# A four-layer graph network on one core: the second norm's squares move to ScalarE, and a score enters the first layer's gather

## The reference

```python
x = _layernorm(x + _L0_gnn_ref(x, adj, ...))   # (x Wq)(x Wk)^T times adj^T, row-normalized, times x Wv
x = _layernorm(x + _L1_gnn_ref(x, adj, ...))   # D^-1/2 adj D^-1/2 x W + b
x = _layernorm(x + _L2_gnn_ref(x, adj, ...))   # three gated steps: a = adj h; z, r sigmoids, tanh; h = (1-z) h + z hv
x = _layernorm(x + _L3_gnn_ref(x, adj, ...))   # masked attention of 8 heads, softmax, output projection
```

## Time and profile before

| what | us |
|---|---|
| median of 3 executions | 2118.96 |
| lowest and highest | 2114.54, 2122.32 |
| the profiled execution, its own time | 2114.17 |
| its span in the trace | 2112.4 |
| TensorE busy | 2027.2 |
| VectorE busy | 1570.5 |
| ScalarE busy | 1253.7 |
| GpSimd busy | 1032.5 |

### The profile page before, as it was taken

One profiled execution on the slowest core, in us unless ns is written; L12 is line 12 of the kernel. 1 busy time (PEld: TensorE's weight loads), 2 busy tenths in 40 slices (PEclk: granted clock), 3 DMA queues, 4 the chain that ended last, 5 costly groups with the idle time before them and its releaser, 6 DMA issues.

```text
span 2112.4 us, 34482 instructions
## 1 busy us (share of the span) xinstructions
PE 2027.2 (96%) x12214; PEld 1632.8 (77%) x12214; DVE 1570.5 (74%) x3442; ACT 1253.7 (59%) x2501; POOL 1032.5 (49%) x1153
## 2 busy tenths in 40 slices
PE   6889999999999999999999999999999999999986
PEld 5667787877878787787877878787787877878764
DVE  5567777777777778777777777778777777877756
ACT  3335647566575656646566575656657566565745
POOL 3123645446364554545445463554535555454546
PEclk8999999999999999999999999999999999999999
DMA  4003022120211203112120212213012120302212
GB/s 135 1 20 70 21 51 51 41 71 21 57 35 48 63 22 71 39 41 51 41 71 21 64 27 57 54 31 71 30 41 51 41 71 21 70 21 61 51 47 65
DMA packets 65631, 101.14 MB, mean 48 GB/s; under 512 B 11440, under 2 KB 31152, under 8 KB 65456
## 3 DMA queue, kind: packets, MB, share of 16 engines
q1 hardware_dynamic: 65456, 98.87, 18.4%
HBM read 23.34 MB, written 8.39 MB: 15 GB/s over the span
## 4 chain that ended last, share of the span: by engine, by line
PE 88%; DVE 4%; ACT 3%; POOL 2%; issue 2%; SPq 0%; DMA 0%; POOLq 0%; DVEq 0%; ACTq 0%
PE ps L1026 18%; PE ps L1028 17%; PE ps L1027 17%; PE ps L1048 12%; PE ps L1140 10%; PE ps L1160 6%; PE ps L1124 5%; PE ps L1451 2%; ACT fa L449 1%; POOL fa L334 1%; PE ps L1220 1%; PE ps L1253 1%; POOL rsum L328 1%; DVE ra L943 0%; DVE fa L781 0%
## 5 line engine op out<-in xcount | busy, mean ns | idle before, releaser
L328 POOL TENSOR_TENSOR rsum<-esum,mhalf 128x2 f32<-128x2 f32 x256 | 209.9, 820 | 598.6 <-ACT fa L449 598.5
L334 POOL TENSOR_SCALAR fa<-fa,rsum 128x512 f32<-128x512 f32 x512 | 442.1, 875 | 54.5 <-POOL rsum L328 54.5
L781 DVE CUSTOM_DVE_ANT_0 fa<-ps,mask 128x512 f32<-128x512 f32 x512 | 332.2, 686 | 157.3 <-PE ps L1124 152.0
L449 ACT ACTIVATE fa<-fa,nmax 128x512 f32<-128x512 f32 x512 | 367.0, 725 | 48.2 <-DVE nmax L781 48.2
L444 ACT COPY pT<-ps 128x512 f32<-128x512 f32 x480 | 276.8, 583 | 150.3 <-PE ps L1140 148.5
L1140 PE MATMUL ps<-ident,fa 128*128 128x128 f32 x1920 | 287.2, 275 | 14.6 <-POOL fa L334 10.6
L1140 PEld LDWEIGHTS ps<-ident,fa 128*128 128x128 f32 x1920 | 230.4, 141 | 88.1 <-issue 22.7
L768 DVE TENSOR_TENSOR ra<-ps,ra 128x512 fp32r<-128x512 f32 x224 | 150.9, 686 | 181.8 <-ACT ra L591 94.4
L1048 PE MATMUL ps<-adjT,ra 128*128 128x512 f32 x1024 | 261.2, 405 | 8.0 <-DVE ra L943 5.2
L1048 PEld LDWEIGHTS ps<-adjT,ra 128*128 128x128 f32 x1024 | 192.5, 192 | 63.1 <-ACT pT L444 8.3
L323 POOL TENSOR_TENSOR rstd<-veps,mhalf 128x2 f32<-128x2 f32 x128 | 98.0, 771 | 167.9 <-DVE veps L748 167.9
(11 more groups left out here) (197 smaller groups left out, 4682.8 us busy)
## 6 DMA issues: line engine op xcount, KB each, us to landing
ra<-ra SPq DMA_DIRECT2D x512, 128.0 KB, 2.4
fa<-in_x_T SPq DMA_DIRECT2D x17, 512.0 KB, 4.7
fa<-in_x SPq DMA_DIRECT2D x17, 512.0 KB, 3.9
out<-fa SPq DMA_DIRECT2D x15, 512.0 KB, 3.0
fa<-in_L_gnn_w_w SPq DMA_DIRECT2D x3, 512.0 KB, 10.7
adj_n<-in_adj SPq DMA_DIRECT2D x1, 1024.0 KB, 8.1
fa<-in_L_gnn_u_w SPq DMA_DIRECT2D x2, 256.0 KB, 10.0
out<-xn SPq DMA_DIRECT2D x2, 256.0 KB, 2.1
```

The source lines that it names most:

```text
L328: nc.gpsimd.tensor_tensor(rsum[:, 2 * k:2 * k + 2], esum[:, 2 * k:2 * k + 2], mhalf[:, 4:6], ALU.pow).then_inc(rs_r, 1)
L334: nc.gpsimd.tensor_scalar(SC[:, g], SC[:, g], rsum[:, 2 * k + u:2 * k + u + 1], 1.0, ALU.mult, ALU.mult).then_inc(nrm, 1)
L449: nc.scalar.activation(SC[:, s % RING], SC[:, s % RING], ACT.Exp, bias=nmax[:, s:s + 1], scale=-1.0, accum_out=esum[:, s:s + 1]).then_inc( ...
L781: nc.vector.tensor_tensor_reduce(out=SC[:, s % RING], in0=ps[:, (4 if i is not None else lone_bank(k)) + u], in1=mask[:, 2 * (k % 8 // 4) ...
```

## The change

The second norm. For each half of the nodes, the residual sums on VectorE now also give their row sums (xsum). A small operation makes the negative mean over 32 (nmean) and signals x2_m. ScalarE takes Square of x/32 + nmean with a row sum, which is a quarter of the variance (256 squares over 1024), writes the squares into XS, which is free then, and signals x2_q. VectorE adds a quarter of epsilon and GpSimd goes on as before. The bn_stats and bn_aggr of this norm are gone. On ScalarE the four Squares stand behind exponentials(t, 0) and ahead of qk_hi(2) and prob_copy(t, 0, 0).

The first scores. score(0) is issued inside the gather of layer 1, after the 9 matmuls that finish tile q = 0 (and start q = 1), ahead of the other 7. On VectorE the sum of X4 goes ahead of the first norm's normalize, and masked(0) between the two low parts.

The first chunk's second half. back(t, 0, 1) goes into bank 6 instead of bank 0, and so waits for prob_copy(t, 0, 0). The wait for pt_c ahead of the gather falls away, and prob_copy(t, 0, 1) moves behind the casts of HTS. qk_hi(3) and qk_lo(3) move later, qk_lo(2) goes behind both low parts of x2, and the gather that waits for qk_lo(2) has three matmuls of q = 0 placed ahead of that wait. The statistics of X4 move behind the low parts of the first gathered tiles in step j = 0.

```diff
+        xsum = sb("xsum", [P, NT])
+        nmean = sb("nmean", [P, NT])
+        vsum = sb("vsum", [P, NT])
...
-        CHAIN_G, CHAIN_T, CHAIN_O = 2 * 6 + 2 + 8 * STEPS, 4, 4
+        CHAIN_G, CHAIN_T, CHAIN_O = 6 + 4 + 2 + 8 * STEPS, 4, 4
...
         def pt_bank(k, c):
-            if (k, c) == (0, 1):
-                return 0
             return 4 + c if k in (5, 9, 13) else PT_BANK
...
+                if i is not None:
+                    for c in range(2):
+                        act.wait_ge(x2_m, i * 2 + (c + 1))
+                        for s in (2 * c, 2 * c + 1):
+                            ins = nc.scalar.activation(XS[:, s], xg[:, s], ACT.Square, bias=nmean[:, s:s + 1],
+                                                       scale=1.0 / 32, accum_out=vsum[:, s:s + 1])
+                        ins.then_inc(x2_q, 1)
+                if t is not None:
                     qk_hi(2)
                     prob_copy(t, 0, 0)
-                    qk_hi(3)
-                for c in range(2):
-                    if i is not None:
+                if i is not None:
+                    for c in range(2):
                         act.wait_ge(x2_r, i * 2 + (c + 1))
                         copy(XNS[:, H, half(c)], xg[:, half(c)]).then_inc(xn_h, 1)
-                    if t is not None and c == 0:
-                        prob_copy(t, 0, 1)
+                if t is not None:
+                    qk_hi(3)
                 if i is not None:
                     for d in range(DT):
                         act.wait_ge(hT_ps, i * 2 + (d + 1))
@@ -571,6 +580,7 @@
                         act.wait_ge(h_c, i * 2 + (d + 1))
                         copy(HTS[:, H, d], hT[:, d]).then_inc(hT_h, 1)
                 if t is not None:
+                    prob_copy(t, 0, 1)
                     exponentials(t, 1)
...
+                def sums_and_means():
+                    for c in range(2):
+                        dve.wait_ge(o1_ps, i * 2 + (c + 1))
+                        for s in (2 * c, 2 * c + 1):
+                            ins = STT(xg[:, s], natural(2)[:, s], dinv[:, s:s + 1], xg[:, s], ALU.mult, ALU.add,
+                                      accum_out=xsum[:, s:s + 1])
+                        after("g", mark("g", ins))
+                        TS(nmean[:, half(c)], xsum[:, half(c)], -1.0 / (32 * D), None, ALU.mult).then_inc(x2_m, 1)
+                    for c in range(2):
+                        n = mark("g", TS(mv[:, 1, half(c), 0], xsum[:, half(c)], 1.0 / D, None, ALU.mult))
+                    after("g", n)
+                    for c in range(2):
+                        dve.wait_ge(x2_q, i * 2 + (c + 1))
+                        TS(veps[:, 1, half(c)], vsum[:, half(c)], 0.25 * EPS, None, ALU.add).then_inc(ln_v[1], 1)
...
+                if o is not None:
+                    dve.wait_ge(yo_ps, o * 2 + 2)
+                    dve.wait_ge(xc_r, o + 1)
+                    TT(X4, natural(4), X4, ALU.add).then_inc(x4a, 1)
+                if i is not None:
                     normalize(xg, xg, 0, 0, i)
                     normalize(xg, xg, 0, 1, i, x1_r)
                 if first:
                     gate_weights()
-                if o is not None:
-                    dve.wait_ge(yo_ps, o * 2 + 2)
-                    dve.wait_ge(xc_r, o + 1)
-                    TT(X4, natural(4), X4, ALU.add).then_inc(x4a, 1)
                 if i is not None:
                     tile_lo(AB0, 0, 0, t_h, i * 2 + 1, t_l)
+                if t is not None:
+                    masked(0)
+                if i is not None:
                     tile_lo(AB0, 0, 1, t_h, i * 2 + 2, t_l)
-                if t is not None:
-                    masked(0)
                 if i is not None:
                     dve.wait_ge(xb_r, i + 1)
-                    sums_and_statistics(1, o1_ps, dinv, xg)
+                    sums_and_means()
                 if i is not None:
                     normalize(xg, xg, 1, 0, i, x2_r)
                     normalize(xg, xg, 1, 1, i, x2_r)
-                for c in range(2):
-                    if i is not None:
+                if i is not None:
+                    for c in range(2):
                         dve.wait_ge(xn_h, i * 6 + (c + 1))
                         TT(XNS[:, L, half(c)], xg[:, half(c)], f32(XNS[:, H, half(c)]), ALU.subtract).then_inc(xn_l, 1)
-                    if t is not None and c == 0:
-                        qk_lo(2)
-                if t is not None:
+                if t is not None:
+                    qk_lo(2)
                     masked(1)
-                    qk_lo(3)
                 if i is not None:
                     for d in range(DT):
                         dve.wait_ge(hT_h, i * 6 + (d + 1))
                         TT(HTS[:, L, d], hT[:, d], f32(HTS[:, H, d]), ALU.subtract).then_inc(hT_l, 1)
                 if t is not None:
+                    qk_lo(3)
                     masked(2)
-                if o is not None:
-                    dve.wait_ge(x4a, o + 1)
-                    x4_0, x4_1 = stats_of("o", X4, 3, 0), stats_of("o", X4, 3, 1)
...
+                    if o is not None and j == 0:
+                        dve.wait_ge(x4a, o + 1)
+                        x4_0, x4_1 = stats_of("o", X4, 3, 0), stats_of("o", X4, 3, 1)
...
-            def gather(xs, ready, value, signal, second=None, second_value=0):
+            def gather(xs, ready, value, signal, second=None, second_value=0, between=None, score=None):
...
                 node_tile(0, 1)
                 pe.wait_ge(ready, value + 1)
                 if second is not None:
+                    node_tile(0, 2)
+                    node_tile(0, 3, (H,))
                     pe.wait_ge(second, second_value)
                 node_tile(1, 0, (H,))
                 with pe.If(lo_words > 0):
                     for q in range(DT):
                         for s in range(NT):
...
-                node_tile(0, 2)
-                node_tile(0, 3).then_inc(signal, 1)
+                if second is None:
+                    node_tile(0, 2)
+                node_tile(0, 3, (H, L) if second is None else (L,)).then_inc(signal, 1)
+                if between is not None:
+                    score(between)
                 node_tile(1, 0, (L,))
                 for s in range(1, NT):
                     ins = node_tile(1, s)
...
-                    if k == 0:
+                    if k == 0 and c == 0:
...
-                    gather(XNS, x1s_l, i * 2 + 1, t_ps)
-                if t is not None:
+                    gather(XNS, x1s_l, i * 2 + 1, t_ps, between=None if t is None else 0, score=score)
+                elif t is not None:
                     score(0)
...
-                if i is not None:
-                    for s in range(NT):
-                        if s % 2 == 0:
-                            pe.wait_ge(x2_r, i * 2 + (s // 2 + 1))
-                        for d in range(DT):
-                            ins = nc.tensor.transpose(ps[:, 2 + d, s * P:(s + 1) * P], xg[:, s, d * P:(d + 1) * P],
-                                                      ident[:, :])
-                            if s == NT - 1:
-                                ins.then_inc(hT_ps, 1)
+                for c in range(2):
+                    if i is not None:
+                        pe.wait_ge(x2_r, i * 2 + (c + 1))
+                        for s in (2 * c, 2 * c + 1):
+                            for d in range(DT):
+                                ins = nc.tensor.transpose(ps[:, 2 + d, s * P:(s + 1) * P], xg[:, s, d * P:(d + 1) * P],
+                                                          ident[:, :])
+                                if s == NT - 1:
+                                    ins.then_inc(hT_ps, 1)
...
                     if i is not None:
-                        if j == 0 and t is not None:
-                            pe.wait_ge(pt_c, t * TILES + 2)
                         gather(XNS, xn_l, m + 1, a_ps, qk_l if j == 0 and t is not None else None, (t or 0) * 4 + 3)
```

More of the change, by code:

```diff
@@ L168, in gnn_stack @@
         u_ps = sem("u_ps"); u_h = sem("u_h"); u_l = sem("u_l"); o_ps = sem("o_ps")
+        x2_m = sem("x2_means"); x2_q = sem("x2_squared")
         ln_v = [sem(f"var_of_norm_{k}") for k in range(4)]
@@ L920, in body @@
                         TT(XNS[:, L, half(c)], XS[:, half(c)], f32(XNS[:, H, half(c)]), ALU.subtract).then_inc(x1s_l, 1)
-                    normalize(xg, xg, 0, 0, i)
-                    normalize(xg, xg, 0, 1, i, x1_r)
-                if first:
-                    gate_weights()
                 if o is not None:
@@ L929, in body @@
                 if i is not None:
+                    normalize(xg, xg, 0, 0, i)
+                    normalize(xg, xg, 0, 1, i, x1_r)
+                if first:
+                    gate_weights()
+                if i is not None:
                     tile_lo(AB0, 0, 0, t_h, i * 2 + 1, t_l)
-                    tile_lo(AB0, 0, 1, t_h, i * 2 + 2, t_l)
```

1 line of the change is left out of this document (added).

## The result

| | before | after |
|---|---|---|
| median, us | 2117.97 (4 executions) | 2068.74 (4 executions) |
| the profiled execution's span, us | 2112.4 | 2066.8 |
| TensorE's mean granted clock | 0.991 | 0.990 |

The ratio is 0.9768, with a 95% interval of 0.9749 to 0.9786: 49 us less, where 20 were forecast and the range ended at 31. The direction was right, the size was not. Executions of one kernel also differ with the granted clock: over all its executions in this document, the kernel before took 2114.2 to 2116.6 us wherever the clock was 0.991, and 2117.8 to 2122.3 wherever it was 0.988. The medians of before mix the two; the spans of the two profiled executions, at 0.991 and 0.990, differ by 45.6.

A forecast was written before the change was run, and what follows sets the result against it. TensorE, busy 96%, bounds the kernel, with 2.1 us of waits per pass. Gains of 1.12 + 0.27 - 0.1 = 1.3 us over fifteen passes plus 1.0 in pass 0 give 20.5 off: 2093.7, median 2098.5, range 2087 to 2113.

The forecast's parts named there:

- Chain (a): score(0), masks, exponentials, probabilities: score(0) inside the gather removes TensorE's 0.88 us wait at the first probability transposes; 0.1 charged.
- Chain (b): Second norm, first sum to second normalize's end: 5.3 us instead of 6.3; Square 0.5 us; gather starts 1.12 us earlier.
- qk_hi(3) and qk_lo(3): Their later place in the queues: no cost charged, since they feed the second group's stack, 20 us away.
- The statistics of X4: Moved ahead of masked(3): costed at nothing, given VectorE's 26% idle; without cover up to 2.5 us.
- The wait on prob_copy: New TensorE wait of back(t, 0, 1), now in the same bank, for the copy: about 0.5 us, 15 times.
- ScalarE's queue gives most of the gain back: Rival: Squares with accumulator cost 0.73 us, leaving 0.6 us per pass, 10 us in all, 2109; chance 0.17.
- GpSimd's long reciprocal: 1.11 us against 0.79 for a root; 0 to 0.4 lost at back(t, 1, 0), 0.1 taken, 0.0 if contention explains it.
- The sum for the order: Per pass 1.12 + 0.27 - 0.1 = 1.3 us; fifteen passes 19.5, with pass 0 20.5 us.
- The larger gain: Rival: copy 0.6 us earlier, VectorE's low part sets the gather; 1.7 us per pass, 26.5 us, 2092; chance 0.13.
- slower: Rival: product with w1 waits for low part 1 behind the masks, delaying the norm; at 2.2 us per pass 2132; chance 0.05.
- the load of an activation table: Rival: Square needs another table, two loads of 1.283 us per pass on ScalarE ahead of the copy; 2135; chance 0.03.

The follow-up runs named there:

- e1: Kernel before with three unused 16-byte tiles declared where the change declares its new ones, moving ra and other big tiles by 96 bytes: 2098.87 us, ratio 0.9909.
- e4: Kernel before with only score(0) inside the gather, the sum of X4 first on VectorE and masked(0) between the low parts; tiles as before: 2111.70 us, ratio 0.9972.
- e2: Changed kernel with its three new tiles declared last, so all other tiles lie where they lay before: 2087.61 us, ratio 0.9856.
- e7: Kernel before with the second norm rewritten and, on ScalarE, qk_hi(3) behind both casts of x2: 2101.05 us, ratio 0.9912.
- e8: Kernel before with second norm rewritten and score(0) moved, nothing else of the change, tiles as before: 2103.35 us, ratio 0.9922.
- e12: Kernel before with second norm rewritten, score(0) moved and qk_hi(3) behind the casts of x2; tiles as before: 2097.23 us, ratio 0.9902.
- e16: Kernel of e12 with the four statistics of X4 moved behind the low parts of the first gathered tiles: 2093.08 us, ratio 0.9884.
- e18: Changed kernel with the transposes of the first half of x2 issued ahead of back(t, 0, 1): 2069.84 us, ratio 0.9780.
- e3: Kernel before with only the second norm rewritten, new tiles declared last, score(0) still behind the gather: 2113.78 us, ratio 0.9982.

## Why the prediction was wrong, step by step

**The new tiles: the step that failed.** The prediction took the three small tiles for free and did not speak of them. They moved ra, and that was worth 18.9 us (e1; 15.4 to 16.4 between executions of equal clock), 1.1 to 1.2 us per pass, spread over the 4480 matmuls of 512 columns that read ra against adjT or a weight. Nothing in the trace of before shows it as a wait: it is in the 0.233 between two starts, which I had taken for the price of a matmul.

**Chain (a)** was right. The 0.88 ahead of the first transposes is gone, the product with w1 waits for the second low part (666.35 - 663.24 = 3.11 instead of 2.87, so 0.24, where 0.1 was charged). Run e4 confirms that alone it is worth little.

**Chain (b)** was right in size. Groups of the changed kernel's ScalarE:

```profile
L563 ACT ACTIVATE fa<-xn,nmean 128x256 f32<-128x256 f32 x64 | 31.9, 500 | 29.2 <-DVE nmean L785 29.2
```

A Square takes 0.50 us, as taken. In VectorE's timeline of e2 (whose tiles lie as before):

```profile
548.74 0.48 DVE L782 SCALAR_TENSOR_TENSOR xn<-ps,dinv,xn 128x256 f32<-128x256 f32 x1 [1.15 <-PE ps L1056]
...
553.22 0.73 DVE L763 TENSOR_SCALAR xn<-xn,mv,rstd 128x256 f32<-128x256 f32 x2 [0.27 <-POOL rstd L325]
553.87 1.46 DVE L972 TENSOR_TENSOR ra<-xn,ra 128x512 fp32r<-128x512 f32 x2
```

From the first sum to the second normalize's end it is 5.2 us (5.3 forecast, 6.3 before). The gather starts 14.06 - 12.81 = 1.25 earlier (1.12 forecast) and lasts 0.25 less (0.27 forecast). Not all of the 1.25 is the norm's: the first sum comes 0.23 later than before, and from the normalized x2 to the gather it takes 0.66 instead of 1.06, since the casts no longer stand behind qk_hi(3).

**qk_hi(3) and qk_lo(3)**: costed at nothing, with the reason that what they feed is 20 us away. That looked at who waits for them, and not at what is queued behind them. e7 shows that qk_hi(3) ahead of the casts takes back 12.7 us of the norm's gain. With the score moved too it is 6 us (e8, e12). That the sum for this stretch came out was luck in so far: it is right only since the change makes this move, whose worth the prediction had not seen.

**The statistics of X4** were a missed gain. I costed the move at nothing, bounded it by a loss, and charged back(t, 1, 0) with 0.1. In fact the kernel before lost 0.22 there in each pass, and the move gives it back: in e2 the four transposes take 0.36. e16 puts it at 4.1 us.

**The wait on prob_copy**: 0.32 in e2 (qk_of(3) ends at 552.88, the transposes begin at 553.20), where 0.5 was forecast; in the changed kernel it stands in 15 passes, as forecast. e18 shows that it costs nothing. The rival in which ScalarE's queue gives most of the gain back did not come true. The page ScalarE: Activation LUTs of the Trainium skill (rules for kernel authors) puts additions and products on VectorE for their time per element. This case does not bear that out as a rule for a chain: VectorE was the serial engine, and with the squares on ScalarE and qk_hi(3) behind the casts (e7) the kernel is 17 us quicker than before.

**GpSimd's long reciprocal**: 1.11 us before; in e2 it takes 0.70, GpSimd's timeline:

```profile
559.18 0.70 POOL L330 TENSOR_TENSOR rsum<-esum,mhalf 128x2 f32<-128x2 f32 x1 [5.99 <-ACT fa L451]
```

VectorE's subtraction with two SBUF inputs now ends ahead of it, at 558.4. By the page GPSIMD Engine Reference of the Trainium skill (specifications) such an instruction contends with GpSimd for SBUF. The trace of before agrees: of its 256 reciprocals (line 328) the 45 that ran beside a VectorE operation on two SBUF tiles took 1.04 on average, the 195 beside other VectorE operations 0.78, and the 16 beside none 0.71. No run varied this alone.

**The sum for the order.** Forecast 1.3 us per pass, measured 126.16 - 124.14 = 2.02 (e2's pass from 1175.69 to 1299.83): 1.25 up to the gather, 0.25 in it, 0.26 at back(t, 1, 0) and the matmuls behind it, and 0.28 in step j = 1, where the group of transposes that ends the step takes 2.24 instead of 2.52. Against the forecast of 1.3 that is 0.13 more up to the gather, 0.36 more at back(t, 1, 0), which I had charged with 0.1, and the 0.28 of step j = 1, which was not foreseen. That last one comes with the new norm (e3 has it, e4 has not). In step j = 1 of e2 GpSimd's two scalings begin 0.36 earlier than before, and the four VectorE operations beside them take 3.68 instead of 3.93 (means of 12 passes; the same in e3, e7, e8 and e12, and as before in e4). What makes the scalings begin earlier is not shown. With the tiles in their old place the change measures 2087.6 (e2), just inside the range, with a gain for the order half as large again as forecast.

**The rivals' chances.** The larger gain (26.5 us) came nearest for the order alone; slower, and the load of an activation table, did not happen (one load in the trace, as before).

## What to carry to other kernels

Before costing a new tile at nothing, look at what it moves: compare the addresses of the large operands in both programs, and set the spacing of the same untouched matmuls in both traces side by side. Compare executions of equal granted clock where a difference is a few us. When an instruction is moved in a queue, ask what stands behind it as well as who waits for it; the gain of a shorter chain can be held back by one cast that stands behind an unrelated wait. And a group that takes longer than the same group elsewhere (0.58 against 0.36) is a stall even where the list of waits does not name it.

## What the runs showed of the hardware

With fp32r matmuls of 512 columns whose two operands lie in different SBUF tiles, the time from start to start was 0.227 us when the distance between the tiles was a multiple of 256 bytes (medians of each trace 0.227 or 0.228), and 0.230 to 0.234 at remainders of 32, 128, 160, 192 and 224, at a granted clock of 0.987 to 0.992 in all. Over this kernel that is 0.7 to 0.9%. The distance counted, not the byte at which the tile begins; the score matmuls, with both operands in ra, did not change. Matmuls of 256 columns were quickest at other remainders: 0.117 to 0.118 at 32, 192 and 224, 0.120 at 0 and 160. The transposes of 128 columns that read fa against ident took 0.109 with that distance at remainder 160 (before) and at 0 (e1).

GpSimd's power of 128x2 elements took 0.71 with VectorE idle beside it and 1.04 beside a VectorE operation on two SBUF tiles, in the trace of the kernel before.
